# First layer's recurrence: the key product moved ahead, beta times state moved from GpSimd to VectorE, coefficient and output copies spread over the turn

## The reference, cut to what matters

```python
def step(S, inp):                                    # S: batch, block n, i, j
    ...                                              # uw: weights of the two routed blocks, sm: softmax of all
    kn = k_t / (jnp.linalg.norm(k_t, axis=-1, keepdims=True) + 1e-06)
    retrieved = jnp.einsum('bnij,bnj->bni', S, kn)
    delta = v_t - retrieved
    outer = delta[..., :, None] * kn[..., None, :]
    S_upd = jnp.tanh(beta_t[..., None] * S + outer)
    w = uw[..., None, None]
    S_new = (1.0 - w) * S + w * S_upd
    Sq = jnp.einsum('bnij,bj->bni', S_new, q_t)
    block_out = Sq * (Sq * jax.nn.sigmoid(Sq))
    out_t = jnp.einsum('bn,bnd->bd', sm, block_out)
    return (S_new, out_t)
```

## Time and profile before

| what | value |
|---|---|
| median of 3 runs | 9594.64 us (9582.53 to 9597.06) |
| the profiled execution | 9595.29 us, its span 9593.5 us |
| the loop's L731, first and last start | 164.4 and 2610.0 us |
| mean granted clock of TensorE over the span | 0.841 of full speed |

### The profile page before, as it was taken

How to read it: one execution, slowest core, us unless ns; L and a number is a source line. 1 busy time by engine, 2 the same in 40 slices (tenths; PEclk the granted TensorE clock), 3 DMA queues, 4 the chain that set the end, 5 groups by cost and what they waited for, 6 DMA issues and landing times. The chain is left out here.

```text
span 9593.5 us, 242768 instructions
## 1 busy us (share of the span) xinstructions
PE 7189.6 (75%) x91413; PEld 4409.5 (46%) x91543; DVE 6310.2 (66%) x13775; ACT 3257.3 (34%) x5970; POOL 3567.5 (37%) x4941
## 2 busy tenths in 40 slices
PE   4777777877774637457746678888888888888887
PEld 2666666666622222233223244444544445454544
DVE  7555555555557665855584567777777777777776
ACT  2222222222242313223413334444444444444444
POOL 1555555545400000300040045555555555555553
PEclk7888888778887767657765789999999999999999
DMA  0000000000000000000000121111111111111111
GB/s 18 1 1 1 1 1 1 1 1 1 0 5 0 14 0 0 0 1 1 0 0 1 41 89 51 55 51 48 55 49 56 51 54 52 48 52 52 51 55 57
DMA packets 156953, 243.03 MB, mean 25 GB/s; under 512 B 21616, under 2 KB 136848, under 8 KB 150160
## 3 DMA queue, kind: packets, MB, share of 16 engines
q1 hardware_dynamic: 155920, 228.84, 7.7%
HBM read 187.06 MB, written 13.66 MB: 21 GB/s over the span
## 5 line engine op out<-in xcount | busy, mean ns | idle before, releaser
L2656 POOL TENSOR_TENSOR big<-big 128x512 f32<-128x512 f32 x388 | 494.6, 1275 | 1920.0 <-DVE big L2498 1920.0
L2666 POOL TENSOR_TENSOR big<-big 128x512 f32<-128x512 f32 x776 | 1045.7, 1380 | 241.2 <-DMA big<-norms 233.6
L1771 POOL TENSOR_TENSOR small<-big 128x480 f32<-128x480 f32 (+14 forms) x240 | 220.8, 954 | 2192.1 <-ACT big L1529 1872.1
L587 ACT ACTIVATE big<-big 128x128 f32<-128x128 f32 x1024 | 317.1, 310 | 1872.2 <-DVE big L735 1782.2
L2073 PE MATMUL banks<-hidden,big 128*128 128x256 f32 x3104 | 837.6, 404 | 111.9 <-DVE big L2498 41.5
L798 POOL TENSOR_TENSOR big<-big 128x128 f32<-128x128 f32 x1024 | 467.1, 456 | 1220.4 <-DVE big L747 1055.5
L498 PE MATMUL banks<-big,constants_on_chip 128*128 128x128 f32 x2048 | 572.1, 367 | 411.6 <-DVE big L739 407.6
L335 PE MATMUL banks<-big,weights_even 128*128 128x512 f32 (+5 forms) x1152 | 623.0, 694 | 234.3 <-DVE big L1052 45.1
L335 PE MATMUL banks<-big,constants_on_chip 128*128 128x512 f32 (+15 forms) x1088 | 526.1, 636 | 361.1 <-DVE big L1662 191.9
L2116 PEld LDWEIGHTS banks<-big 32*32 32x32 f32 x49152 | 545.4, 104 | 513.2 <-issue 512.7
L2137 PE MATMUL banks<-big,hidden 128*32 128x512 f32 x6144 | 776.8, 600 | 4.4 <-ACT big L2388 4.1
(11 more groups left out here) (348 smaller groups left out, 15293.7 us busy)
## 6 DMA issues: line engine op xcount, KB each, us to landing
big<-norms SPq DMA_DIRECT2D x776, 128.0 KB, 2.9
big<-qk SPq DMA_DIRECT2D x50, 512.0 KB, 4.6
big<-vo SPq DMA_DIRECT2D x25, 1024.0 KB, 6.0
weights_odd<-ffn SPq DMA_DIRECT2D x25, 537.5 KB, 5.6
hidden<-big SPq DMA_DIRECT2D x171, 64.0 KB, 4.2
hidden<-big SPq DMA_DIRECT2D x25, 256.0 KB, 3.5
hidden<-big SPq DMA_DIRECT2D x25, 255.8 KB, 4.2
big<-pairs SPq DMA_DIRECT2D x6, 1024.0 KB, 10.7
```

Source lines behind the costliest of these rows:

```text
L2656: self.nc.gpsimd.tensor_tensor(dst, cos, sin, ALU.add).then_inc(*e.did(("turned_pair", f, name, g)))
L2666: self.nc.gpsimd.tensor_tensor(x, x, u["norms"][:, n, g].unsqueeze(1).broadcast_to([P, 2, QTOK]), ALU.mult).then_inc(*e.did(("scaled", f, ...
```

## The change

Four things, all in this loop. First, on VectorE kT is issued ahead of wT. Second, bS is no longer GpSimd's: VectorE computes it at the end of each step from the state it has just written, for the next step. Third, the head and the tail of the turn are gone: the coefficients are copied and worked out in two halves of 16 steps, one operation behind the `arg` of a step (steps 1 to 7 for the second half of the same turn, 17 to 23 for the first half of the next), and `ko` is computed by GpSimd as next key x (1-w). The outputs lie in two banks, one for each half, and are copied out at steps 7 and 23. What the first turn needs is made ahead of the loop, and the last half of the outputs is copied out behind it. Fourth, on TensorE the output product of step s-1 is issued in step s for s = 0 also, so that nothing of the tail is left there. The buffers are the same but for the second output bank, core.bank[7].

```diff
 def cells_tensor(core, e):
...
+    def read_out(s, label):
+
+        bank, c = u["out_bank"][s // HALF_STEPS], s % HALF_STEPS * BATCH
+        nc.tensor.matmul(bank[:, c:c + BATCH], u["S"][(s + 1) % 2], u["qd_c"][:, s * BATCH:(s + 1) * BATCH],
+                         start=True, stop=True, skip_group_check=True).then_inc(*e.did(label))
+
     with e.turns("time", SEQ // STEPS):
         for s in range(STEPS):
...
             if s > 0:
                 pe.wait_ge(*e.after("S", s - 1, PARTS - 1))
...
+            else:
+                pe.wait_ge(*e.after("S", STEPS - 1, PARTS - 1, back=1))
...
+            read_out((s - 1) % STEPS, ("Sq", (s - 1) % STEPS))
...
-        pe.wait_ge(*e.after("S", STEPS - 1, PARTS - 1))
-        nc.tensor.matmul(out_bank[:, (STEPS - 1) * 4:STEPS * 4], u["S"][0], u["qd_c"][:, (STEPS - 1) * 4:STEPS * 4],
-                         start=True, stop=True, skip_group_check=True).then_inc(*e.did(("Sq", STEPS - 1)))
-        pe.wait_ge(*e.after("outer", STEPS - 2, PARTS - 1))
-        pe.wait_ge(*e.after("xrep", 0))
-        values(0, ("v", 0))
...
 def cells_vector(core, e):
...
-        at = bass.ds(turn * STEPS, STEPS)
-        nc.vector.tensor_copy(u["kn_c"], kn[:, :, at]).then_inc(*e.did("kn_c"))
-        nc.vector.tensor_copy(u["w_c"], wt[:, :, at]).then_inc(*e.did("w_c"))
-        nc.vector.tensor_copy(u["knext_c"], knext[:, :, at]).then_inc(*e.did("knext_c"))
...
-        nc.vector.tensor_scalar(u["om_c"], u["w_c"], -1.0, 1.0, ALU.mult, ALU.add).then_inc(*e.did("om_c"))
-
-        tt(u["kw_c"], u["knext_c"], u["w_c"], ALU.mult).then_inc(*e.did())
-        chain()
-        tt(u["ko_c"], u["knext_c"], u["kw_c"], ALU.subtract).then_inc(*e.did("ko_c"))
-        dve.wait_ge(*e.after("Sq", STEPS - 1, back=1))
-        nc.vector.tensor_scalar(u["qd_c"], u["qd"][:, bass.ds(turn * (STEPS * BATCH), STEPS * BATCH)], 1.0, None,
-                                ALU.mult).then_inc(*e.did("qd_c"))
...
             for h in range(PARTS):
-                dve.wait_ge(*e.after("bS", s))
                 dve.wait_ge(*e.after("outer", s, h))
                 tt(cut(u["arg"], h), cut(u["outer"], h), cut(u["bS"], h), ALU.add).then_inc(*e.did(("arg", s, h)))
+            if s == 1:
+                copy_key(1, second)
+            if s == 2:
+                copy_weight(1, second)
+            if s == 3:
+                rest_of_weight(1, ("om_c", 1))
+            if s == 4:
+                copy_next_key(1, second, ("knext_c", 1))
+            if s == 5:
+                weigh_next_key(1)
+            if s == 6:
+                dve.wait_ge(*e.after("Sq", STEPS - 1))
+                copy_query(1, turn * (STEPS * BATCH) + HALF_STEPS * BATCH, ("qd_c", 1))
+            if s == 7:
+                keep_out(1, bass.ds(back_one + HALF_STEPS, HALF_STEPS), ("out", 1))
+            if s == HALF_STEPS + 1:
+                copy_key(0, first)
...
             for h in range(PARTS):
                 dve.wait_ge(*e.after("T", s, h))
+                tt(cut(u["kT"], h), cut(u["T"], h), spread(u["kw_c"], s, h), ALU.mult).then_inc(*e.did(("kT", s, h)))
                 tt(cut(u["wT"], h), cut(u["T"], h), spread(u["w_c"], s, h), ALU.mult).then_inc(*e.did(("wT", s, h)))
-                tt(cut(u["kT"], h), cut(u["T"], h), spread(u["kw_c"], s, h), ALU.mult).then_inc(*e.did(("kT", s, h)))
...
                 tt(cut(new, h), cut(u["wT"], h), cut(u["aS"], h), ALU.add).then_inc(*e.did(("S", s, h)))
-        dve.wait_ge(*e.after("Sq", STEPS - 1))
-        out = u["sq"][:, 0:TOK].rearrange("p (b t) -> p b t", b=BATCH)[:, :, at]
...
+            ahead = (s + 1) % STEPS
+            if ahead % 4 == 0:
+                dve.wait_ge(*e.after("beta", ahead // 4, back=int(0 < ahead // 4 < G - 2)))
+            dve.wait_ge(*e.after("S", s, PARTS - 1))
+            tt(u["bS"], new, u["beta"][:, ahead, :], ALU.mult).then_inc(*e.did(("bS", ahead)))
+    dve.wait_ge(*e.after("Sq_last"))
+    keep_out(1, slice(SEQ - HALF_STEPS, SEQ), "out_last")
...
 def cells_pool(core, e):
...
+    def rest_of_next_key(h, label):
+        nc.gpsimd.tensor_tensor(u["ko_c"][:, :, half_steps(h)], u["knext_c"][:, :, half_steps(h)],
+                                u["om_c"][:, :, half_steps(h)], ALU.mult).then_inc(*e.did(label))
...
-            nc.gpsimd.tensor_tensor(u["bS"], S, u["beta"][:, s, :], ALU.mult).then_inc(*e.did(("bS", s)))
...
             nc.gpsimd.tensor_tensor(full(u["kS"][s % 2]), full(S), by(u["ko_c"]), ALU.mult).then_inc(*e.did(("kS", s)))
             nc.gpsimd.tensor_tensor(full(u["aS"]), full(S), by(u["om_c"]), ALU.mult).then_inc(*e.did(("aS", s)))
+            if s == 6:
+                pool.wait_ge(*e.after("om_c", 1))
+                pool.wait_ge(*e.after("knext_c", 1))
+                rest_of_next_key(1, ("ko_c", 1))
...
```

More of the change, by code:

```diff
@@ L154 @@
 PARTS = 1
+HALF_STEPS = STEPS // 2
+CELL_TURNS = SEQ // STEPS
 NB = BLK // PARTS
@@ L486, in cells_tensor @@
     pe.wait_ge(*e.after("beta0", G - 1))
+    pe.wait_ge(*e.after("coefficients"))
     values(0, ("v0",))
+    def read_out(s, label):
+        bank, c = u["out_bank"][s // HALF_STEPS], s % HALF_STEPS * BATCH
+        nc.tensor.matmul(bank[:, c:c + BATCH], u["S"][(s + 1) % 2], u["qd_c"][:, s * BATCH:(s + 1) * BATCH],
+                         start=True, stop=True, skip_group_check=True).then_inc(*e.did(label))
     with e.turns("time", SEQ // STEPS):
@@ L502, in cells_tensor @@
                 pe.wait_ge(*e.after("S", s - 1, PARTS - 1))
[L503 to L515, removed]
+            else:
+                pe.wait_ge(*e.after("S", STEPS - 1, PARTS - 1, back=1))
+            if s == 1:
+                pe.wait_ge(*e.after("qd_c", 0, back=1))
+                pe.wait_ge(*e.after("out", 0, back=1))
+            if s == HALF_STEPS + 1:
+                pe.wait_ge(*e.after("qd_c", 1))
+                pe.wait_ge(*e.after("out", 1))
+            read_out((s - 1) % STEPS, ("Sq", (s - 1) % STEPS))
+            if s >= 1:
+                pe.wait_ge(*e.after("outer", s - 1, PARTS - 1))
+            else:
+                pe.wait_ge(*e.after("outer", STEPS - 1, PARTS - 1, back=1))
+            if (s + 1) % 4 == 0:
+                pe.wait_ge(*(e.after("xrep", (s + 1) // 4, back=1) if s + 1 < STEPS else e.after("xrep", 0)))
+            values((s + 1) % STEPS, ("v", (s + 1) % STEPS))
             g, m = (s // 4 - 1) % G, s % 4
@@ L523, in cells_tensor @@
                 mm.then_inc(*e.did(("logits", g)))
-        pe.wait_ge(*e.after("S", STEPS - 1, PARTS - 1))
-        nc.tensor.matmul(out_bank[:, (STEPS - 1) * 4:STEPS * 4], u["S"][0], u["qd_c"][:, (STEPS - 1) * 4:STEPS * 4],
-                         start=True, stop=True, skip_group_check=True).then_inc(*e.did(("Sq", STEPS - 1)))
-        pe.wait_ge(*e.after("outer", STEPS - 2, PARTS - 1))
-        pe.wait_ge(*e.after("xrep", 0))
-        values(0, ("v", 0))
-    for q, label in [(0, ("S", STEPS - 1, PARTS - 1)), (1, ("beta", G - 1)), (2, ("out",))]:
+    pe.wait_ge(*e.after("S", STEPS - 1, PARTS - 1))
+    read_out(STEPS - 1, "Sq_last")
+    for label in [("beta", G - 1), ("out_last",)]:
         pe.wait_ge(*e.after(*label))
@@ L598, in cells_scalar @@
                                      core.bank[5 + g % 2], ACT.Sigmoid).then_inc(*e.did(("beta", g)))
-    act.wait_ge(*e.after("out"))
+    act.wait_ge(*e.after("out_last"))
     for t in range(TILES):
@@ L700, in cells_vector, with copy_key, copy_weight, rest_of_weight @@
     nc.vector.tensor_copy(knext[:, :, 0:SEQ - 1], kn[:, :, 1:SEQ]).then_inc(*e.did())
-    nc.vector.memset(knext[:, :, SEQ - 1:SEQ], 0.0).then_inc(*e.did())
+    nc.vector.memset(knext[:, :, SEQ - 1:SEQ], 0.0).then_inc(*e.did("knext"))
+    for bank in u["out_bank"]:
+        nc.vector.memset(bank[:, 0:HALF_STEPS * BATCH], 0.0).then_inc(*e.did())
+    chain()
+    def copy_key(h, at):
+        nc.vector.tensor_copy(u["kn_c"][:, :, half_steps(h)], kn[:, :, at]).then_inc(*e.did())
+    def copy_weight(h, at):
+        nc.vector.tensor_copy(u["w_c"][:, :, half_steps(h)], wt[:, :, at]).then_inc(*e.did())
+    def rest_of_weight(h, label):
+        chain()
+        nc.vector.tensor_scalar(u["om_c"][:, :, half_steps(h)], u["w_c"][:, :, half_steps(h)], -1.0, 1.0, ALU.mult,
+                                ALU.add).then_inc(*e.did(label))
+    def copy_next_key(h, at, label):
+        nc.vector.tensor_copy(u["knext_c"][:, :, half_steps(h)], knext[:, :, at]).then_inc(*e.did(label))
+    def weigh_next_key(h):
+        chain()
+        tt(u["kw_c"][:, :, half_steps(h)], u["knext_c"][:, :, half_steps(h)], u["w_c"][:, :, half_steps(h)],
+           ALU.mult).then_inc(*e.did())
+    def copy_query(h, start, label):
+        n = HALF_STEPS * BATCH
+        nc.vector.tensor_scalar(u["qd_c"][:, h * n:(h + 1) * n], u["qd"][:, bass.ds(start, n)], 1.0, None,
+                                ALU.mult).then_inc(*e.did(label))
+    def keep_out(h, at, label):
+        out = u["sq"][:, 0:TOK].rearrange("p (b t) -> p b t", b=BATCH)[:, :, at]
```

(48 more changed lines are left out.)

30 lines of the change are left out of this document (26 added, 4 removed).

## The result

The changed kernel takes 9615.78 us (median of 11 runs, 9604.84 to 9626.50), the kernel before 9597.06 us beside it (11 runs, 9576.01 to 9612.65). The ratio is 1.0021, with a 95% interval of 1.0012 to 1.0029: slower by 0.2%, a small difference, for single runs of the two kernels overlap. The forecast was 9616 us and slower as the likeliest sign. The profiled execution has a span of 9617.1 us.

A forecast was written before the change was run, and what follows sets the result against it. A three-engine ring was taken to end each step, a separate gap each turn. Terms of +0.13 and +0.52 made +0.65 us a turn, +21 over 32 turns on 9595.3: 9616 us, range 9595 to 9655.

The forecast's parts named there:

- The ring: Each step's path through three engines; after the change TensorE is no longer last and VectorE's uncontested chain takes 2.047 us.
- the sum: The whole loop, steps of 2.298 us and an edge of 4.92: +0.65 us a turn, +21 us over 32 turns.
- The port: In each step arg comes 12 ns after the POOL's aS and waits it out: 2.298 us in place of 2.047.
- The rival in which arg comes first: In each step arg gets the port before aS: fast steps 2.047 us, 9453 us in all; chance 0.22.
- The edge: From a turn's last state to the next turn's first: 4.92 us, with the 2.98 at the branch staying.
- The clock: TensorE's granted clock over the loop stays at 0.83, the lower level for 0.34 of the time.
- the lower level's term: At the lower clock TensorE's products delay one step of four by 0.19 us: 0.52 us a turn.
- The tanh's term: The tanh of every fourth step takes 0.08 us extra, in 8 steps: 0.64 us a turn.
- The case for which the prediction brought the page in: A longer pause before kT's product counts as too little activity, the whole loop runs at the low clock: 9647 us.
- The copies: The 14 half-size operations behind arg hide before kT and cost nothing; without that cover at most 4.1 us a turn.

The follow-up runs named there:

- bs_in_psum: The changed kernel with bS written to an idle PSUM bank in place of on-chip memory (SBUF); 9408.62 us, ratio 0.979 to the kernel before.
- as_after_outer: The changed kernel with one more wait on the POOL, so that aS waits for the step's outer; 9411.26 us, ratio 0.9792 to the kernel before.
- wt_first: The changed kernel with wT ahead of kT again, nothing else; 9560.78 us, ratio 0.9954 to the kernel before.
- edge_alone: The kernel before with only the turn's head and tail moved, wT still ahead of kT, bS on the POOL; 9549.30 us, ratio 0.9943.
- bs_on_pool: The changed kernel with bS back on the POOL, kT still first; 9593.92 us, ratio 0.9994 to the kernel before.

## Why the prediction was right

**The ring.** That TensorE would no longer end most steps was right: 103 releases in place of 991. That VectorE's own chain would be nearly as long as the old ring was right too; with the port out of the way it is 2.05, the 2.047 of the sum.

**The port.** The sum had kS at 0.372, aS at 0.841 and arg at 0.853 after the state; the trace has 0.37, 0.84 and 0.85. arg takes 0.53 to 0.55 in 614 of 1,024 steps, and in some 190 more the delta is later, arg starts at 0.97 to 0.99 inside aS and takes 0.41 or 0.42, as was also forecast. bs_in_psum and as_after_outer show that the wait is worth some 205 us, each by another way.

The changed kernel holds the same race with the other outcome. In step 16 the POOL has one wait more ahead of kS, for the second half of ko. kS then starts 0.53 after the state and not 0.37, and aS at 0.89:

```profile
1052.65 0.29 DVE L818 TENSOR_TENSOR big<-big 128x128 f32<-128x128 f32 x1
...
1053.50 0.29 DVE L776 TENSOR_TENSOR big<-big 128x128 f32<-128x128 f32 x1
1053.55 0.51 POOL L881 TENSOR_TENSOR big<-big 128x128 f32<-128x128 f32 x1
...
1054.70 0.29 DVE L818 TENSOR_TENSOR big<-big 128x128 f32<-128x128 f32 x1
```

arg at 0.85 comes first, takes 0.29, and the step takes 2.05. So it is in 20 of the 32 turns; in 11 others the delta is late, arg comes at 0.97 or 0.98, behind aS, and the step takes 2.35 or 2.36. The order of these two starts decides within one and the same kernel.

The rival in which arg comes first was put at 9453 with a chance of 0.22. bs_in_psum and as_after_outer, at 9409 and 9411, go beyond it: they free the steps with a late delta too, which the rival kept at 2.30, and in bs_in_psum the loop's clock is 0.88 where the rival had 0.83:

```profile
165.80:2421.60 2255.80, 1865.18 (x10359) 1551.74 (x10487) 1696.65 (x6586) 573.85 (x1535) 909.22 (x2109) 0.88 0.00 1
```

**The edge.** The 2.98 from VectorE's last instruction of a turn to the first of the next stayed. In the step shown it is 2.96; over the 31 edges, from L823 to the next L773, it is 2.96 to 3.24 with a mean of 3.05, where the sum had 2.98 and 0.1 for register instructions. From state to state the edge is 4.90 in the mean, forecast 4.92, and from outer to outer 5.19, forecast as about 5.2.

**The clock, and what was luck.** The prediction left the clock at 0.83, and it is 0.79: the lower level for 0.42 of the loop and not 0.34. So the lower level's term was too small: the steps 1, 5, 9 and so on, a part of which it makes late, stand 0.61 us a turn over 2.298 where the sum had 0.52. Against that stands step 16, which the sum had at 2.298 and which is 0.14 a turn below it. The tanh's term is 0.63, forecast 0.64. That the sum, 0.65 us a turn, met the loop's 21.1 / 32 = 0.66 to a hundredth is thus in part luck: two misses of about 0.1 cancelled.

Why the clock fell is open. The page "TensorE: Matmul & The Clock Gate" ("What's actually happening") of the Trainium skill says that activity lifts the clock. The kernel before (0.83 in 2446 us), the change (0.79 in 2467 us) and bs_in_psum (0.88 in 2256 us) would fit it, for the same products in less time are more activity, but wt_first does not: its loop has these products too, is shorter than that of the kernel before, and stands at 0.79. The case for which the prediction brought the page in, the whole loop at the lower level, did not come.

```profile
166.00:2576.00 2410.00, 1864.81 (x10356) 1676.27 (x10483) 1742.95 (x6585) 573.35 (x1534) 911.22 (x2109) 0.79 0.00 1
```

**The copies.** They cost the change nothing that can be seen. Behind ten of the fourteen the kT product still waits 0.22 to 0.32 for the tanh, in place of 0.38. Behind kw and the copy of the queries no wait is listed, and yet steps 6 and 22, which hold the latter, take 2.29 or 2.30 in every turn. In edge_alone two steps of a turn were longer (step 16, and step 25 at 2.69 or 2.70 in 18 turns), so that this is said of the change alone.

**The parts.** By the loop's length: the edge alone takes 43 us off, kT first adds 45 to that (bs_on_pool), bS on VectorE 19 more (the change). In another order: bS on VectorE adds 8 to edge_alone (wt_first) and kT first 56 more. The 8 is not told from nothing, for the two ratios' intervals overlap. Each of the two parts moves arg or the POOL's work against the other; neither has a price of its own.

## What to carry to other kernels

Where a VectorE instruction with two on-chip operands runs beside the POOL, write down when each asks for the port, to 10 ns, before and after the change; who comes first can outweigh what the change moves. An operand in PSUM, or a wait that makes the engine with slack come second, takes the race away. A product that is issued earlier gains only if what it feeds is what ends the step; here the port ended it.

## What the runs showed of the hardware that was not expected

A port wait of 0.25 us a step can be hidden from every list of waits: the page and the waits count arg as busy for 0.54. VectorE looked busier (70% of the span against 66%), and of the 469 us that it gained 110 are arg's own (L776 482 us, L735 372 us), with the same work; only the instruction's own duration tells. One wait more on the POOL (as_after_outer) made the changed kernel some 2% faster than the kernel before. And VectorE can stand for 0.4 us in the middle of a turn, at the same step in each, with its inputs there (edge_alone, bs_on_pool); the profile names a POOL product that VectorE does not need, and the cause is open.
